# Turning three activations in blocks of 32 by 32 on VectorE, by way of DRAM, in a graph and attention layer

## The chip, the cores and the metric

The kernel runs on one core of a Trainium2 chip. The metric is the device time of one execution in microseconds. TensorE multiplies matrices, VectorE, ScalarE and GpSimd work on rows, and SyncE only issues DMAs. Each engine runs its own list of instructions in order and waits on semaphores.

## The reference

1250 nodes with 1024 features, 40000 edges of eight relations, all in float32:

```
xn = layernorm(x)
u  = xn @ root + bias + sum over r of mean_r(xn @ weight[r])        # relational graph convolution
z  = [u, xn] @ w_gate + b_gate;   h = tanh(u) * z + xn * (1 - z)
o  = linear attention of xn (16 heads, Wq, Wk, Wv), gated by sigmoid(xn @ Wg + bg), then @ Wo
x1 = x + h + o
x1n = layernorm(x1);  i, o, g = gates of x1n @ W_iT, W_oT, W_cT     # one step of an LSTM from zero
out = x1 + o * tanh(i * g)
```

## The kernel before

**Units and stages.** The rows are ten tiles of 128 (the last has 98), the features eight blocks of 128 (`K`), the columns of a weight two halves of 512. One *unit* is one row tile times one half of a weight: for each of eight k, three matmuls of 128x512, since every operand is split in a rounded part and a rest (`aThi`, `aTlo` for activations, `Whi`, `Wlo` for weights). The 38 stages stand in one list: the eight relations, then R, V, K, X, G, Q (whose 24 units have the weight standing and row groups of 384, 384 and 482 moving), then O_0, O_1 (`@ Wo`), C_0, C_1 (`u @ w_gate`, and x1 out of it), I, T, F (the LSTM's gates). "C_1,4" is tile 4 of the second half of stage C. Every engine's list is written by one loop over the units q and steps k; `place` gives a unit's number. Sums are evicted from three PSUM banks in turn, so TensorE's unit q waits until that of q-3 is evicted.

**Turned activations.** The left operand has to stand with features on partitions. Three activations are turned in the course of the kernel: the gated attention rows `og` for stage O, the sums `u` for C, the normalized x1 for I, T and F. At step k=2 of one unit for each tile (`TURN_O_AT`, `u_turn`, `x1_turn`) TensorE does eight 128x128 transposes into the PSUM tile `tp` (`turn_rows`), ScalarE casts that to `aThi` (`hi_turned`), VectorE subtracts to `aTlo` (`lo_turned`). The input's own rows are turned in the same way at the start (`turn_x`).

**What stands around it.** SyncE walks through the units as well: in iteration q it issues the loads for the units ahead, then `store_unit(q - 1)`, which waits until that unit's result is made, then a quarter of the next weight (`load_w`). In O_1 it loads the rows of u (`load_u`, a ring of six) and of xn (`load_tx`, two buffers), and stores tanh(u) - xn made by ScalarE and GpSimd (`store_th`). GpSimd makes these ten tiles before it multiplies and adds the first `cring` tile of C_0. In C_1 VectorE makes x1 of unit q-1 at step k=0 of unit q (`make_x1`: multiply, which frees the bank, add, statistics); SyncE's `store_unit` waits for it by these lines:

```python
                elif kind == C_:
                    sp.wait_ge(x1_made, h * T + i + 1)
```

Then `scale_x1` on VectorE and `normalize_x1` on ScalarE give the normalized halves in `A` and `lnb`.

## Time and profile before

| | |
|---|---|
| time, median of 3 runs | 2199.61 us (2198.78 to 2200.4) |
| the profiled execution | 2199.8 us, its span 2198.0 us |
| TensorE busy | 2182.2 us, 99% of the span |
| VectorE, ScalarE, GpSimd busy | 54%, 20%, 33% |
| DMA | 416.62 MB, mean 190 GB/s |

The span is the time from the first to the last instruction that the profiler saw. Busy times of engines overlap each other, so an engine at 54% costs nothing by itself; what counts is what the busiest one waits for.

### The profile page before, as it was taken

Reading aid. Unit: us, or ns where it says so; the run is one execution under the profiler, and the core shown is the slowest. Engines: PE = TensorE matmul, PEld = TensorE weight load, DVE = VectorE, ACT = ScalarE, POOL = GpSimd, SP = SyncE. Lnnn points to the kernel's source line nnn. Section 1 sums busy time; section 2 is a strip of 40 time slices with the busy share of each in tenths; the row PEclk is TensorE's granted clock in tenths of the full one; section 3 lists DMA queues with packets and bytes.
Section 4 is the critical chain, followed back from the end, with each engine's and each line's share of the span. In section 5 each row is a group of like instructions: output and inputs, shape, how many; then the busy total and the mean of one; then the engine's idle time right before and its main releaser. Section 6 shows DMA issues by size and latency. Waiting matters only on the chain.

```text
span 2198.0 us, 25434 instructions
## 1 busy us (share of the span) xinstructions
PE 2182.2 (99%) x10042; PEld 1768.3 (80%) x10042; DVE 1177.1 (54%) x1605; ACT 439.9 (20%) x618; POOL 718.6 (33%) x597
## 2 busy tenths in 40 slices
PE   8999999999999999999999999999999999999999
PEld 6878888888888888888777787889988888888887
DVE  6331677726666566665765676653432367234233
ACT  3221111211111111100221200112321314121121
POOL 4103002055555555544655355521210453000000
PEclk9999999999999999999999999999999999999999
DMA  7543321456788988784968788853127885013102
GB/s 254 186 131 97 110 85 50 128 199 204 274 284 289 312 294 311 243 265 140 324 230 312 241 296 297 273 178 129 48 78 232 270 284 169 34 35 120 59 35 80
DMA packets 191266, 416.62 MB, mean 190 GB/s; under 512 B 33951, under 2 KB 44772, under 8 KB 191146
## 3 DMA queue, kind: packets, MB, share of 16 engines
q1 hardware_dynamic: 127946, 229.10, 30.8%
q0 software_dynamic: 63200, 185.89, 25.4%
q8 instruction: 79, 1.29, 0.2%
q14 instruction: 41, 0.34, 0.1%
HBM read 352.34 MB, written 103.66 MB: 207 GB/s over the span
## 4 chain that ended last, share of the span: by engine, by line
PE 98%; DVE 1%; DMA 0%; ACT 0%; issue 0%; DVEq 0%; ACTq 0%
PE acc L968 90%; PE acc L963 5%; PE tp L821 1%; PE agg L872 1%; PE misc L857 1%; DVE Wlo L1143 0%; DMA xr<-in_x 0%; PE agg L976 0%; PE acc L976 0%; DVE stats L1155 0%; PE tp L829 0%; PE misc L872 0%; DVE xnb L1170 0%; ACT L1012 0%; DVE aTlo L1148 0%
## 5 line engine op out<-in xcount | busy, mean ns | idle before, releaser
L968 PE MATMUL acc<-Whi,aThi 128*128 128x512 f32 (+1 forms) x2872 | 1138.1, 396 | 2.1 <-DVE Wlo L1143 1.6
L968 PE MATMUL acc<-Whi,aTlo 128*128 128x512 f32 (+1 forms) x2872 | 1131.8, 394 | 0.0
L968 PE MATMUL acc<-Wlo,aThi 128*128 128x512 f32 (+1 forms) x2872 | 1128.3, 393 | 0.0
L968 PEld LDWEIGHTS acc<-Whi,aTlo 128*128 128x128 f32 (+1 forms) x2872 | 532.6, 185 | 133.5
L968 PEld LDWEIGHTS acc<-Wlo,aThi 128*128 128x128 f32 (+1 forms) x2872 | 533.8, 186 | 130.9
L968 PEld LDWEIGHTS acc<-Whi,aThi 128*128 128x128 f32 (+1 forms) x2872 | 532.5, 185 | 132.4 <-DVE Wlo L1143 2.0
L1708 POOL DMA_INDIRECT ring<-y_d,edge x390 | 485.1, 1244 | 428.4 <-DVE U L1339 159.1
L1143 DVE TENSOR_TENSOR Wlo<-Wraw,Whi 128x1024 fp32r<-128x1024 f32 x152 | 186.8, 1232 | 322.3 <-ACT Whi L987 321.9
L999 ACT COPY res<-acc 128x512 f32<-128x512 f32 (+1 forms) x180 | 105.8, 588 | 833.8 <-PE acc L968 810.8
L1339 DVE SCALAR_TENSOR_TENSOR U<-ring,edge,U 128x1024 f32<-128x1024 f32 x180 | 230.3, 1280 | 23.2 <-DMA ring<-y_d,edge 22.8
L1339 DVE SCALAR_TENSOR_TENSOR odd<-ring,edge,odd 128x1024 f32<-128x1024 f32 x170 | 217.5, 1279 | 22.2 <-DMA ring<-y_d,edge 21.8
L987 ACT CAST Whi<-Wraw 128x1024 fp32r<-128x1024 f32 x152 | 158.5, 1046 | 196.2 <-DMA Wraw<-in_L_gnn_w_gate 71.9
L1469 DVE TENSOR_TENSOR res<-acc,bias_sb 128x512 f32<-128x512 f32 x99 | 68.5, 691 | 213.2 <-PE acc L968 123.4
L1695 POOL DMA_INDIRECT slot_d<-table,slot x20 | 21.8, 1088 | 227.9 <-DVEq L1299 222.4
L1045 ACT ACTIVATE res<-res 128x512 f32<-128x512 f32 (+1 forms) x59 | 37.3, 633 | 282.3 <-DVE res L1469 282.3
L1448 DVE SCALAR_TENSOR_TENSOR res<-acc,res 128x512 f32<-128x512 f32 (+3 forms) x44 | 28.0, 637 | 103.9 <-ACT res L1012 103.9
L1148 DVE TENSOR_TENSOR aTlo<-tp,aThi 128x1024 fp32r<-128x1024 f32 (+1 forms) x39 | 46.7, 1198 | 53.7 <-ACT aThi L991 53.7
L963 PE MATMUL acc<-aThi,Whi 128*128 128x384 f32 (+1 forms) x192 | 69.9, 364 | 0.0
L1815 POOL TENSOR_TENSOR og<-og,part 128x384 f32<-128x384 f32 (+1 forms) x32 | 27.7, 876 | 127.8 <-DVE part L1499 127.8
L963 PE MATMUL acc<-aThi,Wlo 128*128 128x384 f32 (+1 forms) x192 | 67.6, 352 | 0.0
L963 PE MATMUL acc<-aTlo,Whi 128*128 128x384 f32 (+1 forms) x192 | 67.5, 352 | 0.0
L1010 ACT ACTIVATE res<-acc 128x512 f32<-128x512 f32 (+3 forms) x44 | 24.5, 556 | 181.2 <-PE acc L968 93.0
(177 smaller groups left out, 1034.8 us busy)
## 6 DMA issues: line engine op xcount, KB each, us to landing
y_d<-res SPq DMA_DIRECT2D x144, 256.0 KB
Wraw<-in_L_gnn_weight SPq DMA_DIRECT2D x64, 512.0 KB, 5.5
Wraw<-in_L_gnn_w_gate SPq DMA_DIRECT2D x16, 512.0 KB, 6.0
ring<-y_d,edge POOLq DMA_INDIRECT x390, 6.3
xr<-in_x SPq DMA_DIRECT2D x9, 512.0 KB, 4.5
xn_d<-xnb SPq DMA_DIRECT2D x9, 512.0 KB, 5.6
xs_d<-xr SPq DMA_DIRECT2D x9, 512.0 KB, 5.6
ur_d<-res SPq DMA_DIRECT2D x18, 256.0 KB
```

Source lines behind the costliest of these rows:

```text
L963: mm = nc.tensor.matmul(to, a[:, s % 2, k, cols], b[:, k, c0:c0 + w], start=start, stop=stop)
L968: mm = nc.tensor.matmul(to, a[:, k, rows(i)], b[:, s % 2, k, :], start=start, stop=stop)
L987: nc.scalar.copy(granule(Whi, n), granule(Wraw, n)).then_inc(w_hi, 1)
L999: nc.scalar.copy(res[0:width(i), q % 3, :], acc[0:width(i), q % 3, :]).then_inc(evac_a, 1)
L1045: nc.scalar.activation(a, a, ACT.Tanh if kind == T_ else ACT.Sigmoid).then_inc(gate_act, 1)
L1143: nc.vector.tensor_tensor(granule(Wlo, n), granule(Wraw, n), granule(Whi, n).bitcast(F32), ALU.subtract).then_inc(w_lo, 1)
L1148: nc.vector.tensor_tensor(aTlo[:, :, rows(t)], turned_rows(width(t)), aThi[:, :, rows(t)].bitcast(F32), ALU.subtract).then_inc(done, 1)
L1339: nc.vector.scalar_tensor_tensor(to, g, scale, to, ALU.mult, ALU.add).then_inc(u_acc, 1)
L1448: nc.vector.scalar_tensor_tensor(a, p, 0.0, a, ALU.max, ALU.add).then_inc(evac_v, 1)
L1469: nc.vector.tensor_tensor(to, p, bias_sb[0:w, n % 2, :], ALU.add).then_inc(evac_v, 1)
L1708: pool.indirect_dma_start(ring[:, j % RING, :], None, a, bass.IndirectOffsetOnAxis(ap=index, axis=0), bounds_check=top - 1, oob_is_err=Fal ...
L1815: nc.gpsimd.tensor_tensor(o, o, part[0:w, a % 2, n, :], ALU.mult).then_inc(gated, 1)
```

## The change

The three activations no longer go through TensorE. The gated rows are stored to `o_d` in three groups and loaded back; the normalized x1 is stored to `x1n_d` and loaded back into `zx1`; u comes from DRAM as before. The loads go by quarters of the columns: quarter a, 256 columns wide, goes to partitions 32a to 32a+31, four blocks of 32 rows side by side, so four DMAs for a row tile (eight for the last). One VectorE transpose in blocks of 32x32 then gives the whole tile with features on partitions, in an order in which k-block j holds features 256a + 32j to 256a + 32j + 31. The rows of `w_gate`, `Wo` and the three LSTM weights are put into that order outside the kernel. The transpose writes `aTraw`, which lies on `aTlo`; the cast and the subtraction read it from there. xn for tanh(u) - xn and the store of that go by quarters too. The turns stand at other units: those of og one later, those of u one earlier, those of x1 one later.

```diff
-TURN_O_AT = {place(Q_, 1, 6 + t): t for t in range(3)}
-TURN_O_AT |= {place(Q_, 1, 10): 3, place(Q_, 1, 11): 4, place(O_, 0, 0): 5}
-TURN_O_AT |= {place(O_, 0, t - 4): t for t in range(6, T)}
+TURN_O_AT = {place(Q_, 1, 7 + t): t for t in range(3)}
+TURN_O_AT |= {place(Q_, 1, 11): 3, place(O_, 0, 0): 4, place(O_, 0, 1): 5}
+TURN_O_AT |= {place(O_, 0, t - 3): t for t in range(6, T)}
+STORE_O_AT = {place(Q_, 1, 6): 0, place(Q_, 1, 10): 1, place(O_, 0, 2): 2}
...
+        aTraw = at(top[0] - up(4 * K * N), "aTraw", [128, K, N])
...
+        def blocks(a):
+
+            return a.rearrange("(m n) f -> n m f", n=32)
...
         def u_turn(q):
-            return turn_at(O_, 1, 2, q)
+            return turn_at(O_, 1, 1, q)
+
+        def x1_norm(q):
+            return turn_at(C_, 1, 1, q)
         def x1_turn(q):
-            return turn_at(C_, 1, 3, q)
+            return turn_at(C_, 1, 4, q)
...
+            def load_quarters(to, of, t, done):
+                for a in range(4):
+                    part = to[32 * a:32 * a + 32, :].rearrange("p (m f) -> p m f", f=QUARTER)
+                    cols = slice(a * QUARTER, (a + 1) * QUARTER)
+                    if t < T - 1:
+                        sp.dma_start(part, blocks(of[rows(t), cols])).then_inc(done, 16)
+                    else:
+                        sp.dma_start(part[:, 0:3, :], blocks(of[t * 128:t * 128 + 96, cols])).then_inc(done, 16)
+                        sp.dma_start(part[:, 3, :], of[TAIL:N, cols]).then_inc(done, 16)
...
+            def store_o(g):
+                sp.wait_ge(gated, reads_to(12 + 4 * g + 3))
+                sp.dma_start(o_d[g * 384:g * 384 + 384, :].rearrange("(t p) n -> p t n", p=128), og[:, 3 * g:3 * g + 3, :]
+                             ).then_inc(rows_st, 16)
+                if g == 2:
+                    sp.dma_start(o_d[rows(T - 1), :], og[0:width(T - 1), T - 1, :]).then_inc(rows_st, 16)
+
+            def load_o(g):
+                sp.wait_ge(rows_st, 16 * (4 if g == 2 else g + 1))
+                if g:
+                    sp.wait_ge(o_turned, 3 * g)
+                for t in group_tiles(g):
+                    load_quarters(og[:, t, :], o_d, t, o_in)
...
-                sp.dma_start(tx[0:width(t), t % 2, :], xn_d[rows(t), :]).then_inc(tx_in[t % 2], 16)
+                load_quarters(tx[:, t % 2, :], xn_d, t, tx_in[t % 2])
...
-                sp.dma_start(th_d[rows(t), :], uio[t][0:width(t), :]).then_inc(th_st[t % TH_SEMS], 16)
+                done = th_st[t % TH_SEMS]
+                for a in range(4):
+                    part = uio[t][32 * a:32 * a + 32, :].rearrange("p (m f) -> p m f", f=QUARTER)
+                    cols = slice(a * QUARTER, (a + 1) * QUARTER)
+                    if t < T - 1:
+                        sp.dma_start(blocks(th_d[rows(t), cols]), part).then_inc(done, 16)
...
-                sp.dma_start(uio[t][0:width(t), :], u_d[rows(t), :]).then_inc(u_in[t % U_SEMS], 16)
+                load_quarters(uio[t], u_d, t, u_in[t % U_SEMS])
...
+            def store_x1n(t):
+                sp.wait_ge(ln2_done, 2 * (t + 1))
+                sp.dma_start(x1n_d[rows(t), half(0)], A[0:width(t), t, :]).then_inc(rows_st, 16)
+                sp.dma_start(x1n_d[rows(t), half(1)], lnb[0:width(t), t % 2, :]).then_inc(rows_st, 16)
+
+            def load_x1n(t):
+                sp.wait_ge(rows_st, 16 * 4 + 32 * (t + 1))
+                if t < 2:
+                    wait_th_stored(sp, 8 + t)
+                else:
+                    sp.wait_ge(x1_turned, t - 1)
+                load_quarters(zx1[:, t % 2, :], x1n_d, t, z_in[t % 2])
...
+                    if q in STORE_O_AT:
+                        store_o(STORE_O_AT[q])
+                    if q - 1 in STORE_O_AT:
+                        load_o(STORE_O_AT[q - 1])
+                    if q == place(O_, 0, 8):
                         load_u(0)
                         load_u(1)
                         load_tx(0)
-                    if q == place(O_, 0, 8):
+                    if q == place(O_, 0, 9):
                         load_u(2)
                         load_tx(1)
-                    t = q - place(O_, 0, 6)
+                    t = q - place(O_, 0, 7)
                     if 3 <= t < U_SEMS:
                         load_u(t)
-                    if U_SEMS <= t - 2 < T:
-                        load_u(t - 2)
+                    if U_SEMS <= t - 1 < T:
+                        load_u(t - 1)
...
                     store_unit(q - 1)
                     if KIND[q - 1] == C_ and STAGE[UNIT[q - 1][0]][2] == 0:
                         store_x1(UNIT[q - 1][1])
+                if x1_norm(q - 3) is not None:
+                    load_x1n(x1_norm(q - 3))
+                if x1_norm(q - 2) is not None:
+                    store_x1n(x1_norm(q - 2))
                 if q < UNITS:
                     for n in load_beside(q):
                         load_w(n)
...
-            def turn_o(t):
-                pe.wait_ge(gated, reads_to(12 + 4 * min(t // 3, 2) + 3))
-                if t:
-                    pe.wait_ge(o_lo, t)
-                turn_rows(lambda k: og[0:width(t), t, k * 128:(k + 1) * 128], width(t)).then_inc(o_turned, 1)
...
-                if k == 2 and q in TURN_O_AT:
-                    turn_o(TURN_O_AT[q])
-                if k == 2 and u_turn(q) is not None:
-                    turn_u(u_turn(q))
-                if k == 2 and x1_turn(q) is not None:
-                    turn_x1(x1_turn(q))
...
             def hi_turned(t, turned, count, done):
                 act.wait_ge(turned, count)
-                nc.scalar.copy(aThi[:, :, rows(t)], turned_rows(width(t))).then_inc(done, 1)
+                nc.scalar.copy(aThi[:, :, rows(t)], aTraw[:, :, rows(t)]).then_inc(done, 1)
...
+            def turn_quarters(of, t, done):
+                of = of.rearrange("p (m j f) -> p j m f", m=4, f=32)
+                if t < T - 1:
+                    nc.vector.transpose(aTraw[:, :, rows(t)], of).then_inc(done, 1)
+                else:
+                    chain(nc.vector.transpose(aTraw[:, :, t * 128:t * 128 + 96], of[:, :, 0:3, :]))
+                    nc.vector.transpose(aTraw[:, :, TAIL:N], of[:, :, 3, :]).then_inc(done, 1)
+
+            def turn_o(t):
+                g = min(t // 3, 2)
+                dve.wait_ge(o_in, 16 * sum(quarter_transfers(p) for p in range(group_tiles(g).stop)))
+                dve.wait_ge(prod, place(Q_, 1, 4 * g + 3) + 1)
+                turn_quarters(og[:, t, :], t, o_turned)
+
+            def turn_u(t):
+                dve.wait_ge(u_in[t % U_SEMS], quarters_in(t, U_SEMS))
+                dve.wait_ge(prod, place(O_, 1, t) + 1)
+                turn_quarters(uio[t], t, u_turned)
+
+            def turn_x1(t):
+                dve.wait_ge(z_in[t % 2], quarters_in(t, 2))
+                dve.wait_ge(prod, place(C_, 1, t) + 1)
+                turn_quarters(zx1[:, t % 2, :], t, x1_turned)
...
+                    if k == 3 and q in TURN_O_AT:
+                        turn_o(TURN_O_AT[q])
                     if k == 5 and q in TURN_O_AT:
                         lo_turned(TURN_O_AT[q], o_hi, TURN_O_AT[q] + 1, o_lo)
+                    if k == 3 and u_turn(q) is not None:
+                        turn_u(u_turn(q))
                     if k == 5 and u_turn(q) is not None:
                         lo_turned(u_turn(q), u_hi, u_turn(q) + 1, u_lo)
-                    if k == 3 and x1_turn(q + 2) is not None:
-                        scale_x1(x1_turn(q + 2))
+                    if k == 3 and x1_turn(q) is not None:
+                        turn_x1(x1_turn(q))
+                    if k == 3 and x1_norm(q) is not None:
+                        scale_x1(x1_norm(q))
...
+        if name in by_quarters:
+            a = np.concatenate([a[0:D].reshape(4, K, 32, D).swapaxes(0, 1).reshape(D, D), a[D:]])
```

## Rows read from the trace of the kernel before

**Rows 1.** page: busy time, and the span in 40 slices
```profile
PE 2182.2 (99%) x10042; PEld 1768.3 (80%) x10042; DVE 1177.1 (54%) x1605; ACT 439.9 (20%) x618; POOL 718.6 (33%) x597
...
PEclk9999999999999999999999999999999999999999
DMA  7543321456788988784968788853127885013102
```

**Rows 2.** tile tp: count, ns min/median/max, first and last start
```profile
L821 PE MATMUL tp<-ident,og x80: 247/272/273, 1576.9 to 1648.5; 128*128 128x128 f32 x72, 98*128 98x98 f32 x8
...
L821 PE MATMUL tp<-ident,uio x80: 247/272/277, 1687.5 to 1746.1; 128*128 128x128 f32 x72, 98*128 98x98 f32 x8
...
L821 PE MATMUL tp<-ident,A x40: 247/272/299, 1812.9 to 1872.1; 128*128 128x128 f32 x36, 98*128 98x98 f32 x4
...
L821 PE MATMUL tp<-ident,lnb x40: 247/272/273, 1813.3 to 1872.4; 128*128 128x128 f32 x36, 98*128 98x98 f32 x4
```

**Rows 3.** chain of waits in order of time: start us, us, what
```profile
1569.57 4.22 PE acc L963 x24
...
1745.66 0.68 PE tp L821 x8
...
1833.39 0.87 PE tp L821 x8
1834.27 5.58 PE acc L968 x24
```

**Rows 4.** timeline of SyncE's issues in C_1: start us, us, what
```profile
1813.49 0.32 SPq L558 DMA_DIRECT2D x_d<-res  x1
...
1814.88 0.43 SPq L658 DMA_DIRECT2D cring<-zx_d  x1
1815.35 0.44 SPq L658 DMA_DIRECT2D cring<-base_d  x1
```

**Rows 5.** view of DMA issues: count, KB each, median us from issue to landing
```profile
og<-g_d SPq DMA_DIRECT2D x6, 768.0 KB, 8.4
...
tx<-xn_d SPq DMA_DIRECT2D x9, 512.0 KB, 7.1
...
cring<-th_d SPq DMA_DIRECT2D x18, 256.0 KB, 4.2
...
Wraw<-in_L_mix_Wo SPq DMA_DIRECT2D x8, 512.0 KB, 4.9
...
edge<-slot_d SPq DMA_DIRECT2D x2, 40.0 KB, 1.7
```

**Rows 6.** timeline of VectorE in C_1
```profile
1800.68 0.69 DVE L1519 TENSOR_TENSOR res<-acc,cring 128x512 f32<-128x512 f32 x1 [3.41 <-PE acc L968]
1801.40 0.69 DVE L1521 TENSOR_TENSOR res<-res,cring 128x512 f32<-128x512 f32 x1
...
1803.52 0.16 DVE L1536 RECIPROCAL x_scale<-x_scale 128x1 f32<-128x1 f32 x1 [0.27 <-ACT x_scale L1023]
...
1804.36 0.16 DVE L1540 SCALAR_TENSOR_TENSOR x_scale<-x_scale 128x1 f32<-128x1 f32 x1
```

**Rows 7.** groups by line and shape: count, busy us, mean ns, idle before
```profile
L1143 DVE TENSOR_TENSOR Wlo<-Wraw,Whi 128x1024 fp32r<-128x1024 f32 x152 | 186.8, 1232 | 322.3 <-ACT Whi L987 321.9
...
L1148 DVE TENSOR_TENSOR aTlo<-tp,aThi 128x1024 fp32r<-128x1024 f32 x35 | 42.8, 1224 | 46.6 <-ACT aThi L991 46.6
...
L991 ACT CAST aThi<-tp 128x1024 fp32r<-128x1024 f32 x35 | 35.5, 1014 | 76.1 <-PE tp L821 76.1
...
L1337 DVE TENSOR_SCALAR U<-ring,edge 128x1024 f32<-128x1024 f32 x20 | 15.5, 777 | 13.0 <-DMA ring<-y_d,edge 13.0
```

**Rows 8.** timelines of GpSimd in Q_1 and C_0, and of VectorE in C_0
```profile
1570.67 1.01 POOL L1815 TENSOR_TENSOR og<-og,part 128x384 f32<-128x384 f32 x1 [3.86 <-DVE part L1499]
...
1748.30 2.40 POOL L1820 TENSOR_TENSOR uio<-uio,tx 98x1024 f32<-98x1024 f32 x1 [3.67 <-ACT uio L1017]
...
1753.41 0.69 DVE L1519 TENSOR_TENSOR A<-acc,cring 128x512 f32<-128x512 f32 x1 [10.95 <-POOL cring L1826]
```

More of the change, by code:

```diff
@@ L344, in build @@
         lnb = at(M + 38912, "lnb", [128, 2, H])
+        zx1 = at(M + 43008, "zx1", [128, 2, D])
         fx = at(M, "fx", [128, 3, H])
@@ L367, in build @@
             sem(n) for n in ("ln_var", "ln_root", "ln_done", "xs_made", "x_turned", "x_hi", "x_lo"))
+        z_in = [sem(f"z_in{i}") for i in range(2)]
+        rows_st = sem("rows_st")
+        o_in = sem("o_in")
         edges_in, edges_made, tail_made, codes_st, samples_in = (
@@ L403, in build @@
         gate_act, cell, cell_th, out_made = (sem(n) for n in ("gate_act", "cell", "cell_th", "out_made"))
-        f_in = [sem(f"f_in{i}") for i in range(3)]
         def source_of(s):
@@ L441, in with_halves, with quarter_transfers, quarters_in @@
             return t + 2
+        def quarter_transfers(t):
+            return 8 if t == T - 1 else 4
+        def quarters_in(t, places):
+            return 16 * sum(quarter_transfers(p) for p in range(t % places, t + 1, places))
+        def blocks(a):
+            return a.rearrange("(m n) f -> n m f", n=32)
         def x_tiles(i):
@@ L502, in final_sums, with f_count @@
             return (agg[:, 0, :] if e else acc[:, FINAL % 3, :])[0:width(T - 1), 0:H // 2]
+        def f_count(n):
+            return 48 * len(range(n % 3, 2 * T, 3)) + 16 * (n // 3 + 1)
         def gate_count(q):
@@ L638, in store_th @@
                     wait_th_stored(sp, t - TH_SEMS)
-                sp.dma_start(th_d[rows(t), :], uio[t][0:width(t), :]).then_inc(th_st[t % TH_SEMS], 16)
+                done = th_st[t % TH_SEMS]
[5 more added lines that the diff above has]
+                    else:
+                        sp.dma_start(blocks(th_d[t * 128:t * 128 + 96, cols]), part[:, 0:3, :]).then_inc(done, 16)
+                        rest = N - t * 128 - 96
+                        sp.dma_start(th_d[N - rest:N, cols],
+                                     uio[t][32 * a + 32 - rest:32 * a + 32, 3 * QUARTER:4 * QUARTER]).then_inc(done, 16)
             def load_u(t):
@@ L673, in load_f @@
                     sp.wait_ge(x1_st, 16 * T)
-                sp.dma_start(fx[0:width(t), n % 3, :], x1_d[rows(t), half(h)]).then_inc(f_in[n % 3], 16)
+                sp.dma_start(fx[0:width(t), n % 3, :], x1_d[rows(t), half(h)]).then_inc(c_in[n % 3], 16)
             def general_sums():
@@ L776, in _ @@
                         load_xs(h, i)
-                    if q == place(O_, 0, 7):
+                    if q in STORE_O_AT:
[3 more added lines that the diff above has]
+                    if q == place(O_, 0, 8):
                         load_u(0)
@@ L987, in hi_w, with hi_x @@
                 nc.scalar.copy(granule(Whi, n), granule(Wraw, n)).then_inc(w_hi, 1)
+            def hi_x(t):
+                act.wait_ge(x_turned, with_halves(t))
+                nc.scalar.copy(aThi[:, :, rows(t)], turned_rows(width(t))).then_inc(x_hi, 1)
             def hi_turned(t, turned, count, done):
                 act.wait_ge(turned, count)
-                nc.scalar.copy(aThi[:, :, rows(t)], turned_rows(width(t))).then_inc(done, 1)
+                nc.scalar.copy(aThi[:, :, rows(t)], aTraw[:, :, rows(t)]).then_inc(done, 1)
             def evict(q):
@@ L1124, in _ @@
                     if k == 4 and x1_turn(q) is not None:
-                        act.wait_ge(prod, place(C_, 1, x1_turn(q)) + 1)
                         hi_turned(x1_turn(q), x1_turned, x1_turn(q) + 1, x1_hi)
-                    if k == 1 and x1_turn(q + 2) is not None:
-                        root_x1(x1_turn(q + 2))
-                    if k == 6 and x1_turn(q + 2) is not None:
-                        normalize_x1(x1_turn(q + 2))
+                    if k == 1 and x1_norm(q) is not None:
+                        root_x1(x1_norm(q))
+                    if k == 6 and x1_norm(q) is not None:
+                        normalize_x1(x1_norm(q))
         @block.vector
```

50 lines of the change are left out of this document (20 added, 30 removed).

## The prediction

> **What bounds the kernel now.** I read the page first: TensorE is busy for 2182.2 of 2198.0 us at the full granted clock [rows 1], so only time taken from its queue, or stalls put into it, can move the end. The view of the tile `tp` then gives what the change takes from it: 240 transposes for the gated rows, u and x1 [rows 2]. The chain of waits in order of time shows what they cost: eight transposes stand for 0.87 us between pieces of 24 matmuls at 5.57 us (one unit, 0.232 us a matmul), and for 0.68 us in the last row tile [rows 3]. SyncE's issues [rows 4], the landings [rows 5], VectorE's order in a unit of C_1 [rows 6], durations [rows 7] and four single rows of late work [rows 8] are for the other side of the sum: what the new route makes wait.
>
> **What is removed.** 27 full sets x 0.87 + 3 x 0.68 = 25.5 us of TensorE's time [rows 2, 3]. The matmuls stay as they are; the weights' rows are reordered outside the kernel, so their DMAs keep their shape. ScalarE's cast and VectorE's subtraction read SBUF in place of PSUM: the same subtraction on weights, which reads SBUF, takes 1.23 us against 1.22 [rows 7]. No change; were the cast slower by some tenths, ScalarE, little busy, would not feel it.
>
> **What is added on VectorE.** 30 transposes of 128x1024 f32. No row shows one. Below stands a one-input operation of the same shape, 0.78 us; above, the two-input one, 1.23 us [rows 7]. I take 1.2, as the blocks are short runs. Its 36 us lie beside TensorE's work, VectorE being busy 1177.1 of 2198.0 us [rows 1]; the cost is only where it stands in VectorE's queue and what it waits for.
>
> **What is added on the queues.** A load or store of a row tile becomes four issues (eight for the last tile). SyncE issues back to back every 0.47 us [rows 4], so 1.9 us where 0.47 stood. Three places are checked.
>
> *x1's rows, the term that decides.* In unit q of C_1, VectorE first makes x1 of unit q-1, then waits (step k=3) for the four loads of tile q-4. SyncE issues those loads in its iteration q, and only behind `store_unit(q-1)`, which waits for that same x1. So each unit of C_1 from the fourth holds, in series on VectorE, a full trip of a DMA; SyncE cannot run ahead. One link, from x1 made to the next x1 made:
> - the store of x1, 0.32 us, and the gap: 0.4 [rows 4];
> - four loads of 128 KB, from the first issue to the last landing. Not shown. Below: three spacings of 0.47 and the 1.7 us of a small load, 3.1. Above: 7.1, the tx load in traffic. The nearest is a load of 512 KB in one piece, 4.9 [rows 5]. I take 4.9;
> - the transpose, 1.2;
> - the cast 1.01 and the subtraction 1.22, 2.3 with gaps (the 1.0 us of five small operations of `scale_x1` lie under the cast [rows 6]); in C_1,4, 6 and 8 a `Wlo` granule stands ahead of the subtraction and adds 1.2 [rows 7];
> - multiply and add of the next x1: 1.4 [rows 6].
> That is 10.2 us, or 11.4 with a granule, where TensorE needs 5.57. TensorE has three banks: unit q+3 waits for the eviction of q (the multiply). With zero at the start of C_1,4: x1 of C_1,3 is made at 1.5, its load has landed at 6.8, the subtraction ends at 11.5, the eviction of C_1,4 at 12.2. Then 22.4, 33.8, 44.0, 55.4, 65.6 for C_1,5 to 9, and 75.8 for I_0,0. TensorE would start I_0,3 at 9 x 5.57 = 50.1 and starts it at 75.8: 25.7 us lost. From there no store ties SyncE to VectorE, but SyncE waits for the store of each normalized tile (4.2, as a 256 KB transfer [rows 5]) before it loads it: tile 7 has landed at 78.2, tile 8 at 84.8, tile 9, with eight issues, at 93.3, and I_0,4, 5 and 6 start 1.0, 1.2 and 2.7 us late. Together 30.6 us. By the ends of the landing, 3.1 and 7.1, the mean link is 8.8 or 12.8 (10.6 with 4.9) and the loss about 17 or 52.
>
> *The gated rows.* Group 0 is gated at 1571.7 (1570.67 + 1.01 [rows 8]), 0.5 us into Q_1,5, which starts nine matmuls of 0.176 behind 1569.57 [rows 3]. The store of 1.5 MB meets idle DMA engines [rows 1]; between 4.9 (512 KB) and 8.4 (768 KB behind others [rows 5]) I take 6.6: landed at 1578.4. Twelve issues, 5.6 us, and 2.5 for the last: 1586.5. VectorE has stood at its transpose since 1582.4 (Q_1,7, k=3), and behind it are the subtraction, `attend` and `elu_high` of Q_1,7, which TensorE's read-out wants at 1589. With 1.2 + 2.3 + 1.1 + 0.6 it comes at about 1592: 3 us lost. Group 1 by the same count loses 1. Group 2 has twenty issues and holds VectorE some 10 us in O_0,3, but the three banks cover two units there and it comes out even. I take 4; with 8.4 for each store it is near 11, with 4.9 nothing.
>
> *SyncE's queue ahead of C_0.* In O_1,4 to O_1,7 an iteration now has 14 issues (18 with u's last tile): 1 for xs, 4 u, 4 th, 4 tx, 1 base. At 0.47 that is 6.6 us (8.5) against 5.57. SyncE falls some 6 us behind by C_0,0 and issues the eight loads of the last tx tile at 9.1 us into it; they land at 16, GpSimd's 2.4 follows, then the 2.7 until VectorE can make the first x1 [rows 8] and 0.7 for its multiply: 21.8. TensorE wants that bank at 16.7, three units on. In the kernel before the multiply ended at 1754.1 and C_0,3 started at 1756.1 (from 1745.66 [rows 3]: two units, less six matmuls of the first, plus the set), 2.0 us to spare. I take 4 of the 5.1, since some issues in a row are shorter; if they all took the 0.32 of the first in a row, 14 would need 4.5 and nothing is lost; the upper end is 9.
>
> **Sum.** 2199.8 (the profiled execution, 0.2 above the median of the runs; 1.8 of it lie around its span) - 25.5 + 30.6 + 4 + 4 = 2212.9. Against the median: 2212.7, given as 2213.
>
> **A rule against it.** While x1's rows go round, TensorE stands still for 4 to 6 us in each of five units. The trace never shows that in mid-kernel: its granted clock stays in the top tenth in every slice [rows 1]. The Trainium skill, "TensorE: Matmul & The Clock Gate", section "Why this matters for your kernels", advises against idle gaps of some us between bursts of matmuls, since the clock then halves. This trace cannot show it. By a row, a unit at half clock would take 11.1 us in place of 5.57, just above my link of 10.2 to 11.4: so while the loop is the bound little is added, and the loss comes at its end.
>
> **Rivals.**
> - *The loads are quick and the loss stays small* (other side). Place: the same loop. With links of mean P the loss is about 6P - 33 us (12.2 + 6P - 50.1, and 5 behind it), at the other two places nothing. Break-even with the 25.5 is at P = 9.8, if nothing else stalls. The 1.7 us of small loads speaks for it, the 4.9 of every lone 512 KB load against. At P = 8.8 (landing 3.1) the count of above gives 17: 2191 to 2195.
> - *No loss at all*: were SyncE ahead of VectorE, the 25.5 would come back whole, 2174. The order of the code speaks against: issue and wait stand behind the same x1.
> - *The clock falls.* The gaps bring 1.2 GHz. Units then need 11.1 us; with the ones after the loop still slow I count 2 to 4 units x 5.57 = 11 to 22 on top: 2224 to 2235.
> - *SyncE or the DMA engines are the bound.* 1 KB pieces in a stretch where the engines are already at 7 to 8 tenths [rows 1], landings as long as the 7.1 of tx: 52 in place of 31, 9 and 11 at the other places: up to 2245.
> - *The change does not do what it says*: TensorE keeps transposes. Not possible by the diff, but for the 80 of the input's rows, which it leaves.
>
> **How the numbers follow.** Forecast, the loop costs 25 to 38 us and the rest 4 to 12: 0.50, with 2203 to 2224. Quick loads: 0.20, of which half end within 0.2% of before (2195.2 to 2204.0, about what the measurement can tell from no change). No loss: 0.07. The clock: 0.12. Queue or DMA engines bound: 0.11. Faster: 0.10 + 0.07 = 0.17, and 0.02 from the loop's low end; within 0.2%: 0.10 + 0.04; slower: the rest, 0.67. The range goes from the quick loads' 2190 to 2236, leaving out the no-loss case and most of the DMA-bound one.
>
> **What would show it.** In the profile after: no `tp` group but the input's; TensorE idle 30 to 45 us in mid-kernel, most of it from C_1,9 to I_0,3, five gaps of 4 to 6 us with VectorE's eviction as releaser; the transpose rows of VectorE released by the DMA into `zx1`, waiting 4 to 5 us in each of seven units; links of 10 to 11.5 us between stores of x1 by SyncE. Gaps of 2 to 5 us at the read-outs near Q_1,8 and O_0,0, one near C_0,3. The prediction is wrong if quarter loads land within 3.5 us of the first issue, if a transpose takes 2 us or more, or if the granted clock drops in the gaps.

## The result, and the profile after

The changed kernel takes 2247.2 us (median of 4 runs, 2245.9 to 2249.1) against 2199.7 for the kernel before on the same chip: ratio 1.0217, interval 1.0199 to 1.0235. It is 47.5 us slower. The forecast was 2213, the range 2190 to 2236: the direction is right, and the size is outside the range.

The page of the profiled execution, which has a span of 2244.9 us (busy times, then the span in 40 slices):

```profile
PE 2178.9 (97%) x9802; PEld 1759.8 (78%) x9802; DVE 1212.2 (54%) x1638; ACT 440.2 (20%) x618; POOL 722.7 (32%) x597
...
PE   8999999999999999999999999999999696999999
...
PEclk9999999999999999999999999999999897999999
DMA  6543323275888888857878788741489874313112
```

Against [rows 1], 240 matmul records are gone and VectorE has 35 us more, as foreseen; TensorE is now idle for 66 us where it was idle for 16, and its granted clock leaves the top tenth in two slices. The tile `aTraw` shows the transposes, at 1.24 us each (count, ns min/median/max, first and last start):

```profile
L1220 DVE STREAM_TRANSPOSE aTraw<-og x9: 1233/1236/1246, 1587.5 to 1657.0; 128x1024 f32<-128x1024 f32 x9
L1220 DVE STREAM_TRANSPOSE aTraw<-uio x9: 1234/1235/1237, 1685.9 to 1735.9; 128x1024 f32<-128x1024 f32 x9
L1220 DVE STREAM_TRANSPOSE aTraw<-zx x9: 1236/1246/1247, 1839.1 to 1928.9; 128x1024 f32<-128x1024 f32 x9
```

To see where the time went, I took the start of each unit's first matmul in both traces and compared the lengths. A unit of O, C or I without stall and without transposes takes 5.56 us (a unit of Q with weight standing 4.9 to 6.2). What is above that, in the profiled execution:

| place | units | lost | forecast |
|---|---|---|---|
| gated rows | Q_1,8 11.93; Q_1,9 6.41; O_0,5 7.93; O_0,6 7.15 | 10.3 | 4 |
| ahead of C_0 | C_0,2 22.76; C_0,3 8.43 | 20.1 | 4 |
| x1's loop | C_1,6 6.75; C_1,7 11.37; C_1,8 13.94; C_1,9 11.58; I_0,0 14.29; I_0,1 10.35; I_0,2 11.78; I_0,3 7.65; I_0,4 5.66 | 43.3 | 30.6 |

73.7 us are lost. By the lengths of the units the 30 sets of transposes took 26.0 (0.89 each, 0.71 for a last tile; the forecast's 25.5 goes by 0.87 and 0.68), and a stall of 1.0 of the kernel before in C_1,5 is gone. That leaves 46.7 of the 46.9 by which the two traces stand apart at I_0,5 and to the end; the rest are tenths in units that the table leaves out.

**The loop.** The waits between 1820 and 1915 us (who for whom, us in total, times, longest):

```profile
ACT lnb L1101 <- DVE aTraw L1220: 61.4, 6, 12.2
...
DVE aTraw L1220 <- DMA zx<-x1n_d: 24.1, 6, 5.1
...
PE acc L1030 <- DVE res L1609: 19.4, 5, 5.8
```

The second and third lines were foreseen. The first was not: ScalarE's normalization of the next tile waits for VectorE's transpose of an earlier one. The waiting line, `act.wait_ge(x1_turned, t - 1)`, is the same in both kernels; but what counts `x1_turned` up was TensorE's transpose, and is now VectorE's, which comes only behind a landing. The chain in order of time shows what that does in one link (start us, us, what):

```profile
1848.80 0.32 SPq L604
1849.22 0.38 SPq L563
...
1850.60 3.04 DMA zx<-x1n_d
1853.67 1.26 DVE aTraw L1220
1855.01 0.81 ACT lnb L1101
1855.82 0.70 ACT A L1101
...
1858.73 0.69 DVE res L1609
1859.45 1.05 DVE res L1611
1860.52 0.32 SPq L604
```

From x1 made at 1848.78 to the next at 1860.50 there are 11.7 us. Store and gap 0.4, landing 4.4 from the first issue (1849.22 to 1853.64), transpose 1.26, **ScalarE's two halves of the normalization 1.5**, cast and subtraction 2.2, multiply and add 1.75. The ends of L1611 stand 16.0, 11.7, 13.9, 11.6, 13.0 and 11.4 us apart, where the forecast had 10.2 and, with a `Wlo` granule, 11.4. The 16.0 of the first are a granule, a landing of 5.8 from the first issue, and two operations of `scale_x1` on one column that took 1.37 and 1.16 us in place of 0.23 and 0.17.

**The gated rows.** VectorE stands at its transpose for 4.72 us in Q_1,7, nearly as forecast (4.1). TensorE waits for VectorE's last step of the read-out and then runs slowly (TensorE's timeline):

```profile
1592.60 1.64 PE L963 MATMUL agg<-kv,res 128*128 128x130 f32 x6 [3.42 <-DVE res L1538]
...
1595.24 0.60 PE L1025 MATMUL acc<-aThi,Whi 128*128 128x482 f32 x1
1595.64 0.60 PE L1025 MATMUL acc<-aTlo,Whi 128*128 128x482 f32 x1
...
1598.58 0.38 PE L1025 MATMUL acc<-aThi,Whi 128*128 128x482 f32 x1
1598.80 0.38 PE L1025 MATMUL acc<-aTlo,Whi 128*128 128x482 f32 x1
```

The starts are 0.40 us apart at 1595 and 0.22 again at 1598.6. The view by stretches has the reason (stretch, us, PE, PEld, DVE, ACT, POOL busy with counts, granted clock, DMA share, GB/s):

```profile
1584.00:1588.80 4.80, 4.80 (x27) 4.35 (x25) 1.25 (x1) 0.01 (x1) 0.00 (x0) 1.00 0.57 128
1588.80:1592.60 3.80, 0.38 (x3) 0.03 (x1) 2.66 (x6) 2.89 (x4) 0.53 (x1) 0.84 0.01 2
1592.60:1598.00 5.40, 5.40 (x16) 4.75 (x17) 4.16 (x6) 1.10 (x2) 1.47 (x2) 0.50 0.00 0
```

A gap of 3.4 us brings the granted clock down to 0.50, that is from 2.4 to 1.2 GHz, for the 5.4 us after it. By that the gap costs about ten matmuls x 0.18 = 1.8 us more than itself; the six short ones of the read-out take longer too, so that Q_1,8 has lost 6.0 for a gap of 3.4. Group 2's store, with 2.0 MB, is the longest wait of the part (chain in order of time):

```profile
1626.43 9.46 DMA o_d<-og
...
1644.77 3.97 DMA og<-o_d
1648.77 1.26 DVE aTraw L1220
```

VectorE has stood at this transpose for 13.9 us, and TensorE for 2.2 of them, at the end of O_0,5. Behind that gap the clock is at 0.50 once more (stretch, columns as above), and this is all of the 1.6 that O_0,6 has lost:

```profile
1653.00:1656.20 3.20, 3.19 (x8) 2.52 (x9) 3.19 (x3) 1.05 (x1) 0.00 (x0) 0.50 0.46 164
```

**Ahead of C_0.** The chain again, down to the matmuls that end TensorE's idle time:

```profile
1746.56 0.46 SPq L563
...
1750.87 1.16 SPq L704
...
1753.85 0.48 SPq L565
...
1757.68 2.69 DMA tx<-xn_d
...
1760.51 2.34 POOL uio L1915
1762.85 1.23 POOL cring L1920
...
1765.49 0.70 DVE A L1609
1766.24 3.78 PE acc L1030 x8
```

From 1698 us on SyncE issues with hardly a pause, and an iteration of it takes longer than a unit: its stores into `base_d`, one in each, start at 1698.44, 1706.38, 1713.63, 1720.87 and 1730.92. That is 7.2 to 7.9 us, and 10.0 with the last tile of u, where the forecast had 6.6 and 8.5; single issues take up to 1.16 us here (L704 above), one 1.83. The eight loads of the last tx tile go out from 1753.85 and have landed at 1760.4; the forecast had 9.1 and 16 us into C_0,0, which starts at 1732.4, so 1741.5 and 1748.4. The 12 us between are what its 5.1 lacks to the 17.2 of C_0,2. What follows the landing goes as forecast. The eight matmuls at the end are the first of C_0,3. They take 0.47 us each, double, after a gap of 17 us; this is the 2.9 lost in C_0,3.

### The profile page after: what moved, and what is told of

Its sections match the earlier page's. It is cut to its first block, busy times and chain, and to the rows that moved or that the text cites. A ratio compares the mean times of both kernels' runs of the same rounds, so it can differ in the third digit from the quotient of the medians.

```text
span 2244.9 us, 25183 instructions
## 1 busy us (share of the span) xinstructions
PE 2178.9 (97%) x9802; PEld 1759.8 (78%) x9802; DVE 1212.2 (54%) x1638; ACT 440.2 (20%) x618; POOL 722.7 (32%) x597
## 3 DMA queue, kind: packets, MB, share of 16 engines
q8 instruction: 77, 1.26, 0.2%
## 4 chain that ended last, share of the span: by engine, by line
PE 83%; issue 5%; DMA 4%; SPq 4%; DVE 3%; POOL 1%; ACT 1%; DVEq 0%; POOLq 0%; ACTq 0%
PE acc L1030 81%; SPq L563 2%; DMA zx<-x1n_d 1%; POOL og L1911 1%; DMA bias_sb<-xs_d 1%; DMA o_d<-og 1%; SPq L704 1%; DVE aTraw L1220 1%; PE misc L948 1%; DMA og<-o_d 0%; PE tp L912 0%; DVE Wlo L1204 0%; DVE res L1611 0%; SPq L604 0%; SPq L566 0%
## 5 line engine op out<-in xcount | busy, mean ns | idle before, releaser
L1915 POOL TENSOR_TENSOR uio<-uio,tx 128x1024 f32<-128x1024 f32 x10 | 24.1, 2406 | 113.4 <-ACT uio L1082 70.1
```

## The experiments

Times are medians, ratios stand against the kernel before on the same chip. "Lost" counts in the way of the table above.

### Is it x1's loop?

x1's rows go through TensorE again, the other two activations by the new route. The edit restores `turn_x1` and takes out `store_x1n` and `load_x1n`:

```diff
-                if x1_norm(q - 3) is not None:
-                    load_x1n(x1_norm(q - 3))
-                if x1_norm(q - 2) is not None:
-                    store_x1n(x1_norm(q - 2))
+                if k == 2 and x1_turn(q) is not None:
+                    turn_x1(x1_turn(q))
```

> x1 alone goes back to TensorE's transposes (C_1, one unit earlier, weights of the LSTM in plain order); gated rows and u stay on the new route. Counted from unit to unit in the two traces, the changed kernel loses 43.3 us between C_1,6 and I_0,4. Theory A (the series of x1 made, store, load, transpose, next x1 on VectorE): those 43.3 go, eight sets of transposes cost 8.5 again and the 1.0 us stall of before in C_1,5 comes back: 2213 us (2210 to 2217). Theory B (the loss in C_1 is carried over from the queues that were late in C_0, so that the order inside C_1 matters little): over 2230.

2212.0 us (2210.8 to 2213.4), ratio 1.0060 (1.0037 to 1.0082). The loop loses nothing beyond its transposes, 35.2 us come back.

### ScalarE's wait

```diff
                 if t >= 2:
-                    act.wait_ge(x1_turned, t - 1)
+                    act.wait_ge(rows_st, 64 + 32 * (t - 1))
```

`lnb` has two buffers. It may be written again when its store has landed; the wait for the transpose is stricter than that.

> One wait of ScalarE changed: before it writes the normalized tile t into lnb and A, it waits until the store of tile t-2 to DRAM has landed, not until tile t-2 has been transposed. Theory A1 (in each link ScalarE's two normalizing activations, 0.82 and 0.70 us, stand between the transpose and the cast because of that wait): seven links get 1.5 us shorter, 2236 to 2238 us. Theory A2 (only the DMA trip and VectorE's own work make the link, ScalarE's order costs nothing): within 2 us of 2247.

2235.4 us (2235.0 to 2235.8), ratio 1.0166 (1.0137 to 1.0196). The loop loses 32.3 in place of 43.3, that is seven links x 1.5 us. The chain of this kernel, in one link:

```profile
1848.53 0.38 SPq L563
...
1849.92 2.91 DMA zx<-x1n_d
1852.86 1.26 DVE aTraw L1220
1854.13 1.05 ACT aThi L1057
...
1856.36 0.69 DVE res L1609
1857.08 0.70 DVE res L1611
1857.79 0.32 SPq L604
```

The cast follows the transpose at once. x1 is made 9.7 us after the one before (1848.10 to 1857.78), the next links are 11.5 and 10.7: the forecast's loop. That the total is so near its 30.6 us is in part luck. I_0,3 starts 29.2 us late where 25.7 were forecast, since the first landing took 7.6 us and not 4.9; the six links from the eviction of C_1,4 to that of I_0,0 have a mean of 10.4 (forecast 10.6). Behind that 3.1 are lost where 4.9 were forecast, and not by the waits that the forecast had there: 2.9 of them are I_0,3, which starts at 1909.6 and runs at a granted clock of 0.50 until 1915.8.

### The turn one unit later

On top of that the turn of tile t moves from C_1,t+4 to C_1,t+5, so that a landing has a whole unit.

```diff
-            return turn_at(C_, 1, 4, q)
+            return turn_at(C_, 1, 5, q)
```

> As guard_by_store, and VectorE turns tile q-5 in unit q, not q-4; SyncE's order of issues is as before. Then the load behind x1 of unit q-1 is wanted only in unit q+1, a link of some 10 us spans two units, 5.0 to 5.8 us each. Theory A: the loss between C_1,6 and I_0,4 falls from 43.3 to between 0 and 10 us, the upper end because SyncE still waits for each tile's store (about 4 us) before it issues its four loads and the next two stores, some 7 us for a tile: 2204 to 2214 us. Theory B (SyncE's 11 issues in a unit, or VectorE's transposes, are the bound): over 2230.

2210.0 us (2208.0 to 2210.3), ratio 1.0048 (1.0026 to 1.0071). The loop loses 6.4. The round trip is the same; it has only left VectorE's path between two tiles of x1.

A variant puts a tile's store ahead of the load of the tile before in SyncE's queue, each on its own semaphore.

> As the kernel in which x1's rows are turned one unit later and ScalarE waits for the store (2210.0 us), and in SyncE's queue a tile's store now stands ahead of the load of the tile before, each waiting on a semaphore of its own parity. Theory A (what is left of the loop's loss, about 6 us, is the load's wait in SyncE's queue holding the next tile's store back): the loop loses 0 to 3, and the time is 2204 to 2207. Theory B (what is left is the landing time of the four loads): no change, 2209 to 2211.

2210.6 us (2208.0 to 2211.9), ratio 1.0047: no change, 6.3 lost in the loop. The store's place is not what is left here.

### The gated rows one unit later

```diff
-TURN_O_AT = {place(Q_, 1, 7 + t): t for t in range(3)}
-TURN_O_AT |= {place(Q_, 1, 11): 3, place(O_, 0, 0): 4, place(O_, 0, 1): 5}
-TURN_O_AT |= {place(O_, 0, t - 3): t for t in range(6, T)}
+TURN_O_AT = {place(Q_, 1, 8 + t): t for t in range(3)}
+TURN_O_AT |= {place(O_, 0, 0): 3, place(O_, 0, 1): 4, place(O_, 0, 2): 5}
+TURN_O_AT |= {place(O_, 0, t - 2): t for t in range(6, T)}
...
-                dve.wait_ge(o_in, 16 * sum(quarter_transfers(p) for p in range(group_tiles(g).stop)))
+                dve.wait_ge(o_in[t - 3 * g], 64 * (g + 1) if t < T - 1 else 16 + 128)
```

> Each tile of gated rows is turned one unit later, and its turn waits for its own four loads, not for the last load of its group of three. Theory A (the group's last quarters land 4 to 6 us after the turn's place): of the 10.3 us lost in Q_1,8, Q_1,9, O_0,5 and O_0,6, 1 to 3 are left, and the time is 2238 to 2241. Theory B (the rows' way through DRAM is late by several units whatever the wait): the stalls move with the turn and the time stays within 2 us of 2247.

2242.2 us, ratio 1.0192 (1.0163 to 1.0222). All of the 10.3 is gone (Q_1,8 takes 5.94, O_0,5 and O_0,6 5.56), more than expected; of that, 5.0 reach the end. In this execution the loop loses 49.1, 6 more. The landing in its first link takes 6.5 us from the last issue in place of 4.4 (the DMA pieces of the two chains, at 1823.90 and 1834.68). The earlier start of C_1 doesn't explain it: in the nine kernels of this document that leave the loop as it is, it loses 43.3 to 49.3, the changed kernel least, and 45.6 where C_1 starts earliest (1789.9 us, `u_long_pieces_one_issue`). How much of this spread is chance in single executions, and what the rest is, stays open; a step of a few us that a kernel with the loop in place gains elsewhere can be lost in it.

### u by whole rows and TensorE

```diff
-                load_quarters(uio[t], u_d, t, u_in[t % U_SEMS])
+                sp.dma_start(uio[t][0:width(t), :], u_d[rows(t), :]).then_inc(u_in[t % U_SEMS], 16)
```

> u alone goes back to TensorE's transposes, and with it u, xn and tanh(u) - xn move in whole rows, one DMA of 4 KB pieces where four of 1 KB pieces stood; gated rows and x1 stay on the new route. The changed kernel loses 20.1 us at C_0,2 and C_0,3. Theory C (SyncE's queue and the DMA engines are full from O_1,3 on, GpSimd gets xn too late): those 20.1 go, 8.5 of transposes come back: 2235.6 us (2232 to 2239). Theory D (the late point is the gated rows' third group, which delays all that follows): 2250 or more.

u, tx and th are carried by one DMA of whole rows for each tile, as before the change, and TensorE turns u. 2238.2 us, ratio 1.0179 (1.0149 to 1.0209). The 20.1 in C_0 are gone entirely, for 8.5 us of transposes; the loop loses 45.0 here.

### SyncE's queue or the DMA engines?

Six kernels part what the new route changes in u's stretch: 14 issues a unit, pieces of 1 KB, and DMAs that reach only 32 partitions. The first two move issues to ScalarE's queue (`store_th`, then also `load_tx`):

```diff
+                    if k == 7 and 0 <= q - place(O_, 1, 3) < T:
+                        store_th(q - place(O_, 1, 3))
```

> The stores of tanh(u) minus x are issued from ScalarE's queue, not SyncE's; pieces, bytes and order of the rest as in the changed kernel. Theory Q (SyncE's issue queue sets the 17.2 us stall in C_0,2): in u's stretch SyncE issues ten DMAs a unit in place of fourteen, 10 x 0.47 = 4.7 us, less than a unit's 5.57, so it no longer falls behind; the 20.1 us lost in C_0 fall to at most 5, and the time is 2227 to 2232. Theory D (the DMA engines themselves are full, because the quarters' 1 KB pieces take more of their time per byte): the same packets are carried, so the time stays within 3 us of 2247.

> The loads of x's rows beside u's turn, as well as the stores of tanh(u) minus x, are issued from ScalarE's queue; SyncE is left with six DMAs a unit in u's stretch. Theory Q: as with the stores alone, 2227 to 2232, or a little less. Theory D: within 3 us of 2247. If the stores alone change half of it and this one the rest, both queue and engines count.

2246.9 us (ratio 1.0214) and 2249.2 us (1.0224). The loss in C_0 falls to 12.8 in the first, and the loop takes back 5.9 of the 7.3; in the second it is 17.6. Both times are those of theory D, but the first not for its reason: the loss in C_0 has fallen, though not to theory Q's 5, and a larger loss in the loop hides it. So the queue counts, but something stands close behind it. In the second, ScalarE's own queue is the late one: it issues in groups from 1744.7 to 1764.6, with pauses of 1.8 to 2.1 us between them, its issues for the last tx tile end at 1755.9, and they have landed at 1759.1, only 1.3 us earlier than in the changed kernel.

The other four carry u, tx and th of nine tiles in another form and turn whatever arrives, so the order of u's elements is left out. The transfer is one of these:

```diff
+# u_long_pieces: 32 whole rows, four DMAs
+sp.dma_start(to[32 * a:32 * a + 32, :], of[t * 128 + 32 * a:t * 128 + 32 * a + 32, :]).then_inc(done, 16)
+# u_long_pieces_one_issue: 128 whole rows
+sp.dma_start(to[:, :], of[rows(t), :]).then_inc(done, 16)
+# u_columns_four_issues: a quarter of the columns in 128 partitions, four DMAs
+sp.dma_start(to[:, c], of[rows(t), c]).then_inc(done, 16)
+# u_short_pieces_one_issue: 512 pieces of 1 KB in 128 partitions
+out_ = of[rows(t), :].rearrange("(m a) (b f) -> (a b) m f", m=4, f=QUARTER)
+sp.dma_start(to[:, :].rearrange("p (m f) -> p m f", f=QUARTER), out_).then_inc(done, 16)
```

> For nine of the ten tiles, u, x beside it and tanh(u) minus x are carried by four DMAs a tile as in the changed kernel, but each is 32 whole rows (4 KB pieces) and not 128 rows' quarters (1 KB pieces); the turn by VectorE and all else stay (what is turned is then permuted, so this kernel leaves the right order of u out). Same issues, same bytes, longer pieces. Theory D (the DMA engines are full with 1 KB pieces): the 20.1 us lost in C_0,2 and C_0,3 fall to at most 3, the time is 2227 to 2230. Theory Q (SyncE's 14 issues a unit): the loss stays within 3 us of 20.1, the time of 2247.

> As u_long_pieces, but one DMA a tile in place of four, so SyncE issues 5 a unit and not 14. Both theories: no loss in C_0, 2226 to 2229. If u_long_pieces keeps part of the loss, this one shows the queue's share of it by the difference.

> As u_long_pieces (nine of ten tiles, the right order of u left out), but each of a tile's four DMAs carries 128 rows' quarters of the columns into 128 partitions: 14 issues a unit and 1 KB pieces as in the changed kernel, 128 partitions and not 32. Theory P (a DMA over 32 partitions moves slowly): the 20.1 us lost in C_0,2 and C_0,3 fall by 8 or more, the time to 2239 or less. Theory Q (the number of issues): loss within 3 of 20, time within 3 of 2247.

> As u_long_pieces_one_issue (5 issues a unit, 128 partitions, the right order of u left out), but a tile's rows are laid so that its one DMA is of 512 pieces of 1 KB. Theory Q: as with 4 KB pieces, 1 to 4 us lost in C_0, 2231 to 2234. Theory D (1 KB pieces fill the engines): the loss is 10 or more, 2240 or more.

They took 2246.4, 2231.3, 2244.5 and 2236.8 us in the order of their names above (ratios 1.0214, 1.0145, 1.0204, 1.0169, each known to 0.002). Few met their expectations in full: `u_long_pieces` has theory Q's time and, within 0.1 us, its loss, the second is 2 us over its range, `u_columns_four_issues` has theory Q's time with a loss between the two theories, and `u_short_pieces_one_issue` is nearer to Q's 1 to 4 us of loss than to D's 10, and within neither. The stretch 1690 to 1745 us, in the order changed kernel, u_long_pieces, u_long_pieces_one_issue, u_columns_four_issues, u_short_pieces_one_issue (columns as above):

```profile
1690.00:1745.00 55.00, 55.00 (x239) 44.10 (x238) 31.68 (x32) 21.60 (x22) 16.25 (x7) 1.00 1.00 278
```

```profile
1690.00:1745.00 55.00, 55.00 (x239) 44.01 (x238) 31.98 (x32) 21.06 (x22) 18.78 (x8) 1.00 0.99 297
```

```profile
1690.00:1745.00 55.00, 55.00 (x239) 44.05 (x238) 32.10 (x31) 21.76 (x22) 20.04 (x8) 1.00 0.97 335
```

```profile
1690.00:1745.00 55.00, 55.00 (x239) 44.05 (x238) 33.99 (x30) 20.50 (x21) 18.75 (x7) 1.00 0.88 282
```

```profile
1690.00:1745.00 55.00, 55.00 (x240) 44.01 (x239) 33.21 (x31) 21.76 (x22) 20.34 (x8) 1.00 1.00 323
```

The share of the DMA engines (the number before the last) is near 1 in all but the fourth, so it doesn't part them; what differs is how much they move. The kernel before moved 309 GB/s here in units of 6.45 us, 1.99 MB a unit, which at 5.56 us would be 358 GB/s (an estimate): none of the five gets there, and the last ones only nearly. Mean packet times in this stretch, from the packets of the traces:

| kernel | issues a unit | piece | partitions | packet of u, tx, th | GB/s | lost in C_0,2 and 3 |
|---|---|---|---|---|---|---|
| changed | 14 | 1 KB | 32 | 62 ns | 278 | 20.1 |
| u_long_pieces | 14 | 4 KB | 32 | 216 ns | 297 | 17.0 |
| u_columns_four_issues | 14 | 1 KB | 128 | 51 ns | 282 | 14.1 |
| u_short_pieces_one_issue | 5 | 1 KB | 128 | 50 ns | 323 | 5.2 |
| u_long_pieces_one_issue | 5 | 4 KB | 128 | 167 ns | 335 | 1.1 |

Read downward from the first row by way of the third, one property changes at a time: reaching 128 partitions in place of 32 gives back 6.0, five issues in place of 14 give 8.9, pieces of 4 KB in place of 1 KB give 4.1, and 1.1 is left. All three count, and the number of issues counts most. By another order the shares would differ somewhat: over 32 partitions, longer pieces give 3.1 and not 4.1. The losses come from one execution each; in the six kernels that carry u, tx and th as the changed one does, from SyncE, the loss in C_0 lies between 19.2 and 20.7. The times tell less, since the loop takes back part of each gain: the 6.0 are 2.7 us there, within the noise of the two medians.

That the packets are slower on the mean over 32 partitions (62 against 51 ns, 216 against 167; the median of the first pair is 46 in both, and the second pair differs in its issues too) agrees with the Trainium skill, "SBUF — State Buffer", section "Door 1: The DMA port swizzle (why `[64,N]` ≈ `[32,N]`)", by which 32 adjacent partitions reach only half of the ports.

### Blocks laid out in DRAM

Could all three stay on VectorE? Here x, tanh(u) - x and x1 stand in DRAM in the order of the blocks, so that loads into `tx` and `zx1` and the store of th are one DMA a tile; x's and x1's stores and the reads of th by `cring` take the 1 KB pieces. The turns are one unit later, as above.

```diff
+        def laid(of, t, a):
+            return of[t * 128 + 32 * a:t * 128 + 32 * a + 32, :].rearrange("n (m f) -> m n f", f=QUARTER)
...
-                sp.dma_start(xn_d[rows(t), :], xnb[0:width(t), t % XS, :]).then_inc(xn_st[t % XS], 16)
+                for a in range(4):
+                    cols = slice(a * QUARTER, (a + 1) * QUARTER)
+                    sp.dma_start(laid(xn_d, t, a) if t < T - 1 else xn_d[rows(t), cols], xnb[0:width(t), t % XS, cols]
+                                 ).then_inc(xn_st[t % XS], 16)
```

> All three by VectorE. x's rows, tanh(u) minus x and x1's rows are laid in DRAM in the order of the blocks (quarter, row within 32, block, column), so that tx, zx1 and the store of tanh(u) minus x are one DMA a tile with 4 KB pieces; x's stores, x1's stores and the reads of tanh(u) minus x take the 1 KB pieces instead. u's loads stay in quarters. SyncE issues 8 a unit in u's stretch, not 14. x1's and the gated rows' turns are one unit later and a tile's store of x1 stands ahead of the load of the tile before. Theory D and Q both: C_0's 20.1 fall to 0 to 4; x1's loss is 0 to 6 of 43.3, gated rows' 5 of 10.3: 2247.2 - 18 - 40 - 5 = 2184, range 2180 to 2192. Rival: the quarters' pieces only move the DMA engines' load into C_0 and the link from x1 to x1 gets longer by its two more stores: 2195 to 2205.

2245.6 us, ratio 1.0209 (1.0192 to 1.0226): some 60 us above what was expected. It loses 14.4 us by the end of Y0_1,5 already, where x's rows are stored, 14.9 in C_0 and 43.1 in the loop. SyncE's timeline shows the stores in the new form:

```profile
1857.48 0.43 SPq L614 DMA_DIRECT2D x_d<-res  x1
1857.96 2.46 SPq L760 DMA_DIRECT2D x1n_d<-A  x2
1860.46 2.96 SPq L760 DMA_DIRECT2D x1n_d<-lnb  x2
1863.53 1.88 SPq L769 DMA_DIRECT2D zx<-x1n_d  x1
```

Of the four issues that write a tile in 1 KB pieces block by block, the first stands for 0.54 us in the queue and the others as a rule for 1.3 to 1.9, where a plain one takes 0.43; the load behind them stands for 1.9. Fewer issues, but most hold SyncE three times as long. The pieces themselves move slowly too. While no other DMA is under way (stretch, columns as above):

```profile
1861.00:1862.00 1.00, 0.00 (x0) 0.00 (x0) 0.96 (x3) 0.22 (x1) 0.00 (x0) 1.00 0.27 92
```

The DMA engines are busy for 0.27 of their time, as much as four of sixteen, and move 92 GB/s; with the quarters of the changed kernel, also 1 KB pieces, it is 0.91 and 277 GB/s (1851 to 1852 us). A rule for it is in the Trainium skill, "DMA: Bandwidth & Descriptors", section "Why a DMA increments its semaphore by 16 and not by 1": the slowest dimension of the access pattern sets over how many DMA engines a DMA is spread, and in this form that dimension is the four blocks. The 0.27 agrees with that; no run here shows which engines they were, nor whether this is also what holds the queue.

### What beats both kernels

The three edits that helped, together: u by whole rows and TensorE, x1's turn one unit later with ScalarE waiting for the store, the gated rows' turn one unit later with a wait for each tile.

> u turned by TensorE again, x1's rows turned by VectorE one unit later with ScalarE waiting for the store, gated rows turned one unit later with a wait per tile. Adding the three single steps to the changed kernel's 2247.2: -9.0 (u by TensorE), -37.2 (x1 later), -5.0 (gated rows later) gives 2196.0, within 2193 to 2200: faster than the kernel before by about 3.6 us or equal to it. If the steps interfere (x1's loss grows once C_0's stall no longer gives its DMAs time), 2200 to 2206.

2187.9 us (2186.0 to 2188.8), ratio 0.9945 (0.9928 to 0.9961), 8 us less than the sum said. The single steps had been taken with the loop in place, which ate part of each: now the gated rows' 10.3 count and not 5.0, and u's 20.1 - 8.5 = 11.6 and not 9.0, which is 7.9. That reading was made afterwards, and it is not exact: 0.9 of the gated rows' loss is still there, in O_0,6. All three on VectorE with only the two later turns was not run; by 20.1 - 8.5 more it would stand at about 2199.5, an estimate, no faster than the kernel before. With the store ahead of the load as well:

> As turns_later_u_by_pe (2187.9 us), with a tile's store of x1 ahead of the load of the tile before in SyncE's queue, each waiting on its own parity's semaphore. Theory A (the waits for the store of the last tiles, 4.7 and 3.6 us in the chain before I_0, come from four loads being issued first): 2 to 4 us less, 2184 to 2186. Theory B (the landing of the store itself): 2187 to 2189.

2185.4 us (2184.5 to 2189.5), ratio 0.9941 (0.9925 to 0.9958). The profile has 2.9 us lost in the loop against 6.4; by the runs the two kernels are not told apart. The page of this kernel, with a span of 2182.7 us:

```profile
PE 2166.8 (99%) x9882; PEld 1751.9 (80%) x9882; DVE 1203.2 (55%) x1627; ACT 441.6 (20%) x618; POOL 726.3 (33%) x597
...
PEclk9999999999999999999999999999999999999999
```

TensorE has lost the 160 transposes of x1 and the gated rows, it is idle for 15.9 us of the span as it was before the change (15.8), and the clock stays up.

## Why the prediction was wrong

Against the forecast the loop lost 12.7 us more, the gated rows 6.3 and the place ahead of C_0 16.1. Together, 35.1, that is the whole distance between 2212.7 and 2247.2.

- **What is removed**, 25.5 us: right, by the count of matmuls (240 fewer) and the units' lengths (26.0). Neither cast nor subtraction became dearer (1.05 and 1.23 us from SBUF).
- **What is added on VectorE**, 1.2 us for a transpose: 1.24.
- **x1's rows, the term that decides**: the mechanism is right and the term too small, 43.3 for 30.6. The link had one step missing. "One link, from x1 made to the next x1 made" went from the transpose straight to the cast; ScalarE's queue has the next tile's normalization between them, and it waits for `x1_turned`, by a line that the diff leaves alone but whose semaphore it gives to another engine. With that wait on the store the loop loses 32.3, and its links are as forecast (10.4 for 10.6; the landing 4.9 for 4.4 as a rule). The first landing and the end of the loop were not: 29.2 for 25.7 up to I_0,3, 3.1 for 4.9 behind it. In the changed kernel the end cost 2.2, and the waits forecast for I_0,4 to I_0,6 cost 0.1. The missing step had been looked for on VectorE and SyncE, not on ScalarE.
- **The gated rows**, 4 for 10.3. Group 0's arrival came out right (1587.5 for 1586.5) by errors that cancel: the store took 5.3 for 6.6, the twelve issues 6.4 for 5.6, the last landing 4.5 for 2.5. TensorE's gap behind it was right too, 3.4 for 3. Missing were the clock at 0.50 after the gap (the rest of Q_1,8's 6.0 and the 0.3 in Q_1,9), and group 2: its store took 9.46 us, above the 8.4 of the upper end, it held VectorE for 13.9 us and not 10, and "comes out even" became 4.0 in O_0,5 and O_0,6, of which 1.6 are again the clock. Group 1, forecast at 1, lost nothing.
- **SyncE's queue ahead of C_0**, 4 for 20.1, the largest error. The count of issues, 6.6 us a unit, put SyncE 6 us behind. An iteration took 7.2 to 7.9, and the last loads went out and landed 12 us later than forecast. The DMAs moved 278 GB/s where the estimate for a unit of 5.56 us is 358. The prediction had both in one rival with the upper end 9 and did not multiply them out: a row of units, each short of time by its issues and its DMAs. The parted runs give 8.9 to the issues, 6.0 to the 32 partitions, 4.1 to the pieces. The clock in C_0,3 is 2.9 of the 20.1.
- **The clock rival** holds in kind: gaps bring the clock to 0.50. The rule cited from the Trainium skill, "TensorE: Matmul & The Clock Gate", "Why this matters for your kernels", agrees with the trace in Q_1,8 and in C_0,3. The prediction named a fall of the clock as a sign that it is wrong, and it fell in or just after every gap of 2 us or more in this kernel. Its price is small, some 2 (Q_1,8) + 1.6 (O_0,6) + 2.9 (C_0,3) + 1.7 (of I_0,3's 2.1) = about 8 us of 73.7, and not 11 to 22 behind the loop, since while VectorE sets the pace a slow unit costs nothing: in the loop none of VectorE's evictions waited for TensorE.
- **No loss at all** and **quick loads** fell: four quarters landed 4.3 to 5.8 us after the first issue in the seven links of this kernel, and 4.3 to 7.6 in those of the one with ScalarE's wait on the store.
- The signs named: `tp` only for the input, right; TensorE idle 30 to 45 us in mid-kernel, more (50 us more than before, 17 in one piece ahead of C_0); transposes waiting 4 to 5 us for `zx1`, nearly (24.1 in 6, 3.6 to 5.1 each); links of 10 to 11.5, in fact 11.4 to 16.0.

## What to carry to other kernels

When a diff gives a semaphore to another engine, walk the queue of every engine that waits for it, also where the waiting line has not changed: a step of 1.5 us that used to be free stood in each of seven links. Where a round trip over DRAM is put between two steps of one engine, first give it one more unit of distance: that alone was worth 25 us here (2235.4 to 2210.0), as much as all the transposes removed. And before transfers are split, work out a unit's bytes and issues against the unit's time: full queues do not cost in the unit where they fill, but at the next point where somebody waits for the last one.

## What the runs showed of the hardware

- A transpose in 32x32 blocks of 128x1024 f32 takes VectorE 1.24 us, as long as a two-input operation of that shape (1.23).
- After a gap of 3.4 us in TensorE's work the granted clock was 0.50 in the next 5.4 us, after one of 2.2 us (O_0,5) in the next 3.2.
- DMAs over 32 partitions: on the mean 62 ns a packet of 1 KB and 216 of 4 KB in a full stretch, against 51 and 167 over 128. The stretch from 1690 to 1745 us moved 278 to 335 GB/s in the five kernels compared.
- Stores in 1 KB pieces whose slowest dimension is four blocks kept the DMA engines busy for 0.27 of their time at 92 GB/s (`laid_out_in_dram`, 1861 to 1862 us).
- SyncE's issue is not of fixed length: 0.43 us as a rule, 1.3 to 1.9 for most stores in 1 KB pieces block by block, and up to 1.2 for a quarter of th in the stretch ahead of C_0.
